# A state-space layer with a mixture of experts on one core: experts of the next-to-last row placed mostly within the last row's slot, and stages at moments of their own on ScalarE and VectorE

## The reference

```python
h = layernorm(x) * (1 + ca) + sa                  # modulation from silu(c) @ wmod
x = x + ga * state_space(h)
h = layernorm(x) * (1 + cb) + sb
x = x + gb * experts(h)

def state_space(x):
    xn = layernorm(x) * norm_scale + norm_bias
    xb, z = split(xn @ W_in)                      # 512 channels each
    xb = silu(conv3(xb)); dt = softplus(xb @ W_dt + b_dt)
    B, C = xb @ W_B, xb @ W_C                     # 16 states
    h_t = exp(dt_t * A) * h_(t-1) + dt_t * x_t * B_t
    y_t = sum over states of h_t * C_t
    return x + ((y + D * xb) * silu(z)) @ W_out

def experts(x):                                   # 16 experts, inner width 128, 4 of them used per token
    w = routing weights from sigmoid(x @ gate_weight), top 2 of 4 groups, top 4 experts
    return sum over e of w[:, e] * (silu(x @ gate[e]) * (x @ up[e])) @ down[e]
```

## Time and profile before

| | us |
|---|---|
| median of 3 runs | 2831.6 (2829.8 to 2836.8) |
| the profiled execution | 2827.4 |
| its span, first to last instruction | 2825.6 |
| VectorE busy | 2430 (86%) |
| TensorE busy | 2399 (85%) |
| GpSimd busy | 2238 (79%) |
| ScalarE busy | 1564 (55%) |
| start of the first scan | 95.5 |

### The profile page before, as it was taken

One profiled execution on the slowest core, in us unless ns is written; L12 is line 12 of the kernel. 1 busy time (PEld: TensorE's weight loads), 2 busy tenths in 40 slices (PEclk: granted clock), 3 DMA queues, 4 the chain that ended last, 5 costly groups with the idle time before them and its releaser, 6 DMA issues.

```text
span 2825.6 us, 29196 instructions
## 1 busy us (share of the span) xinstructions
PE 2398.6 (85%) x9004; PEld 1685.0 (60%) x9004; DVE 2430.4 (86%) x2482; ACT 1564.0 (55%) x2945; POOL 2237.5 (79%) x1563
## 2 busy tenths in 40 slices
PE   3445698989989898997989899898989989898899
PEld 1212466666756666675666667566666756666678
DVE  2678899989989898999989899998989899898932
ACT  3555665556556556656665665566566556655311
POOL 1577888888888888888888888888888888887922
PEclk7667899999989899999999899998989999899999
DMA  4699899999999999999999999999999999998921
GB/s 111 180 225 232 227 235 242 231 235 237 239 234 231 234 228 237 236 239 234 236 241 232 232 238 235 234 234 234 238 232 235 237 233 237 231 241 220 258 70 49
DMA packets 354510, 626.19 MB, mean 222 GB/s; under 512 B 51488, under 2 KB 162080, under 8 KB 354352
## 3 DMA queue, kind: packets, MB, share of 16 engines
q0 software_dynamic: 72960, 243.30, 45.3%
q1 hardware_dynamic: 281392, 381.01, 42.9%
HBM read 379.25 MB, written 10.06 MB: 138 GB/s over the span
## 4 chain that ended last, share of the span: by engine, by line
PE 40%; DVE 23%; issue 12%; POOL 9%; ACT 8%; DMA 7%; SPq 1%; DVEq 0%; POOLq 0%; ACTq 0%
DVE hbank L700 13%; PE wbank L477 13%; PE mbank L489 6%; PE wbank L419 4%; PE wbank L379 4%; POOL unit L1167 4%; PE wbank L505 4%; PE wbank L367 3%; DMA w_all<-w_scratch 2%; DMA w_scratch<-rows_out 2%; PE wbank L502 2%; DMA gsum<-unit 2%; DVE unit L714 2%; ACT z L823 2%; DVE act L678 2%
## 5 line engine op out<-in xcount | busy, mean ns | idle before, releaser
L1167 POOL TENSOR_TENSOR unit<-dtx,b_bc 128x1024 f32<-128x1024 f32 x512 | 1358.7, 2663 | 10.5 <-DMA b_bc<-bc_scratch 6.3
L700 DVE TENSOR_TENSOR_SCAN hbank<-hbank,unit 128x1024 f32<-128x1024 f32 x512 | 1173.3, 2292 | 103.3 <-ACT hbank L997 94.4
L997 ACT ACTIVATE hbank<-dt,a_neg 128x512 f32<-128x512 f32 x1024 | 669.2, 681 | 332.7 <-DVE unit L714 298.8
L489 PE MATMUL mbank<-down_t,act 128*128 128x256 f32 x2048 | 536.1, 402 | 57.1 <-POOL act L1135 31.2
L1179 POOL DMA_DIRECT2D gsum<-unit x448 | 452.7, 1010 | 161.4 <-DVE unit L714 75.4
L714 DVE TENSOR_TENSOR unit<-hbank,c_bc 128x1024 f32<-128x1024 f32 x448 | 545.8, 1218 | 22.3 <-DMA c_bc<-bc_scratch 1.4
L1135 POOL TENSOR_TENSOR act<-act,w_all 128x512 f32<-128x512 f32 x256 | 360.0, 1406 | 252.2 <-DVE act L678 228.2
L477 PE MATMUL wbank<-h_t,gate_t 128*128 128x256 f32 x2048 | 496.3, 386 | 24.1 <-DVE act L678 12.7
L489 PEld LDWEIGHTS mbank<-down_t,act 128*128 128x128 f32 x2048 | 402.1, 200 | 162.2 <-issue 62.6
L477 PE MATMUL wbank<-h_t,up_t 128*128 128x256 f32 x2048 | 486.9, 381 | 12.9 <-DVE gz L587 11.2
L477 PEld LDWEIGHTS wbank<-h_t,gate_t 128*128 128x128 f32 x2048 | 387.7, 192 | 128.6 <-DVE act L678 27.1
(11 more groups left out here) (122 smaller groups left out, 2400.9 us busy)
## 6 DMA issues: line engine op xcount, KB each, us to landing
gsum<-unit POOLq DMA_DIRECT2D x448, 512.0 KB, 7.5
b_bc<-bc_scratch SPq DMA_DIRECT2D x512, 256.0 KB, 6.3
c_bc<-bc_scratch SPq DMA_DIRECT2D x512, 256.0 KB, 5.5
w_all<-w_scratch SPq DMA_DIRECT2D x256, 256.0 KB, 5.0
ht<-in_L_attn_x_dram SPq DMA_DIRECT2D x16, 512.0 KB, 8.5
w_out<-in_L_attn_W_out_dram SPq DMA_DIRECT2D x16, 512.0 KB, 10.1
ht<-in_L_attn_x_dram POOLq DMA_DIRECT2D x16, 512.0 KB, 10.2
out_dram<-xt SPq DMA_DIRECT2D x16, 512.0 KB, 3.3
```

The lines of the kernel that those rows point to most:

```text
L489: m = eng.matmul(mbank[:, u * H:(u + 1) * H], act[:, (n - 1) % MOE_RING, j, u * P:(u + 1) * P], down_t[:, e, :], start=(e == 0 and u == 0) ...
L700: eng.tensor_tensor_scan(h, h, unit[:, g % RING, :, :].rearrange("p a t -> p (a t)"), 0.0, ALU.mult, ALU.add).then_inc(scanned, 1)
L997: eng.activation(hbank[g % HB][:, a, :], dt[:, 2 * q + a, :], ACT.Exp, scale=a_neg[:, 2 * q + a, n:n + 1]).then_inc(decayed, 1)
L1167: eng.tensor_tensor(unit[:, g % RING, :, :], dtx[:, 2 * q:2 * q + 2, :], b_bc[:, s:s + 1, :].to_broadcast([P, 2, T]), ALU.mult).then_inc(d ...
```

## The change

The change only moves instructions within the queues; the instructions themselves stay the same.

- Row 14's experts are spread over moments 37 to 107 of slot 15 in place of 38 to 131 (`SHORT_EXPERTS_AT`). Those of row 15 start at tail moment 43 in place of 33, behind everything that is placed in the tail.
- `streams`: `load_gb`, `stats`, `weigh`, `load_wo`, `load_ga`, `scale_wo`, `gates` and `silu_last` get other moments. `last_streams` too.
- `streams` takes a table of delays for single stages on one engine. ScalarE takes up `project` 2 moments later and `rows_bc` 1 later, VectorE takes up `mix1` 1 earlier; all other entries are 0.
- SP takes up the experts' DMAs (loads of `w_all`, output of a row) 4 moments late in place of 3 (`W_LAG`).

```diff
@@ -103,11 +103,16 @@
     SLOWEST = 1e-25
     MOE_RING = 2
     EXPERTS_AT = (38, 131)
+    SHORT_EXPERTS_AT = (37, 107)
     EP = E // 2
-    LAST_EXPERTS_AT = (33, 134)
+    LAST_EXPERTS_AT = (43, 124)
     HALVES = 4 * (E + 1)
     EARLY = 4
     ACT_LAG, DVE_LAG, POOL_LAG, SP_LAG = 1, 2, 3, 3
+    W_LAG = 4
+    ACT_LATE = {"project": 2, "stats": 0, "turn": 0, "gates": 0, "silu_first": 0, "silu_last": 0, "rows_bc": 1,
+                "step_sizes0": 0, "step_sizes1": 0, "turn_in": 0, "norms": 0, "weigh": 0}
+    DVE_LATE = {"gates": 0, "silu_first": 0, "silu_last": 0, "mix0": 0, "mix1": -1, "pick": 0}
     TAIL = 14
     HT = T // 2
     W2 = 2 * H
@@ -270,23 +275,25 @@
 
             return q if q < 2 else 2 + (q - 2) + 2 * (row % 2)
 
-        def streams(slot, stage):
+        def streams(slot, stage, late):
+
 
             behind, coming = slot - 1, slot + 1
             plan = [] if slot else [("chunks", 0, 2 * (len(chunks) - EARLY), 4, 40)]
             if behind >= 0:
-                plan += [("mix1", behind, 4, 11, 14), ("load_gb", behind, 1, 54, 56),
-                         ("project", behind, 4, 15, 24), ("stats", behind, 5, 20, 26),
-                         ("turn", behind, 4, 27, 30), ("pick", behind, 5, 30, 32), ("weigh", behind, 2, 36, 37)]
-            plan += [("step_sizes1", slot, 9, 1, 7), ("load_wo", slot, 1, 24, 30), ("load_ga", slot, 1, 23, 26), ("scale_wo", slot, 1, 47, 47),
-                     ("scale_h", slot, 2, 56, 58), ("gates", slot, 9, 36, 42),
+                plan += [("mix1", behind, 4, 11, 14), ("load_gb", behind, 1, 56, 58),
+                         ("project", behind, 4, 15, 24), ("stats", behind, 5, 22, 26),
+                         ("turn", behind, 4, 27, 30), ("pick", behind, 5, 30, 32), ("weigh", behind, 2, 34, 36)]
+            plan += [("step_sizes1", slot, 9, 1, 7), ("load_wo", slot, 1, 33, 42), ("load_ga", slot, 1, 31, 46), ("scale_wo", slot, 1, 48, 48),
+                     ("scale_h", slot, 2, 56, 58), ("gates", slot, 9, 35, 41),
                      ("mix0", slot, 4, 55, 62)]
             if coming < NB:
                 plan += [("load_x", coming, 1, 24, 29), ("norms", coming, 12, 31, 45), ("turn_in", coming, 2, 48, 55),
-                         ("silu_first", coming, 6, 57, 60), ("silu_last", coming, 6, 61, 65),
+                         ("silu_first", coming, 6, 57, 60), ("silu_last", coming, 6, 61, 66),
                          ("rows_bc", coming, 3, 81, 83),
                          ("step_sizes0", coming, 9, 73, 79)]
-            return [Steps(stage[name](row), n, first, final) for name, row, n, first, final in plan if name in stage]
+            return [Steps(stage[name](row), n, first + late.get(name, 0), final + late.get(name, 0))
+                    for name, row, n, first, final in plan if name in stage]
 
         def first_row(stage, begun=None):
 
@@ -298,13 +305,16 @@
         def last_streams(stage):
 
             last = NB - 1
-            plan = [("mix1", last, 4, 5, 5), ("project", last, 4, 6, 6),
-                    ("stats", last, 5, 6, 8), ("turn", last, 4, 16, 18), ("load_gb", last, 1, 21, 26),
-                    ("pick", last, 5, 16, 16), ("weigh", last, 2, 24, 25)]
+            plan = [("mix1", last, 4, 5, 5), ("project", last, 4, 5, 5),
+                    ("stats", last, 5, 6, 8), ("turn", last, 4, 18, 19), ("load_gb", last, 1, 3, 11),
+                    ("pick", last, 5, 13, 18), ("weigh", last, 2, 18, 25)]
             return [Steps(stage[name](row), n, first, final) for name, row, n, first, final in plan if name in stage]
 
         def experts_of(row, gen):
-            return Halves(gen(row), HALVES, *EXPERTS_AT) if 0 <= row < NB else None
+            if not 0 <= row < NB:
+                return None
+
+            return Halves(gen(row), HALVES, *(EXPERTS_AT if row < NB - 2 else SHORT_EXPERTS_AT))
 
         def experts_at(older, young, moment):
 
@@ -779,7 +789,7 @@
-                beside = streams(slot, stage_of) if run else last_streams(stage_of)
+                beside = streams(slot, stage_of, DVE_LATE) if run else last_streams(stage_of)
...
@@ -1036,7 +1046,7 @@
-                beside = streams(slot, stage_of) if run else last_streams(stage_of)
+                beside = streams(slot, stage_of, ACT_LATE) if run else last_streams(stage_of)
...
@@ -1370,7 +1380,7 @@
-                beside = streams(slot, stage_of)
+                beside = streams(slot, stage_of, {})
...
@@ -1378,7 +1388,7 @@
-                    experts_at(older, young, moment - SP_LAG)
+                    experts_at(older, young, moment - W_LAG)
...
```

More of the change, by code:

```diff
@@ L533, in _ @@
                 run = slot < NB
-                beside = streams(slot, stage_of) if run else last_streams(stage_of)
+                beside = streams(slot, stage_of, {}) if run else last_streams(stage_of)
                 young = experts_of(slot - 1, experts) if run else Halves(
```

1 line of the change is left out of this document (removed).

## The result

| | before | after |
|---|---|---|
| median of 8 runs each | 2829.95 (2823.09 to 2836.82) | 2839.38 (2834.62 to 2845.04) |
| ratio, with its 95% interval | | 1.0036 [1.0023, 1.0049] |
| span of the profiled execution | 2825.6 | 2836.5 |
| VectorE, TensorE busy | 2430, 2399 | 2430, 2382 |

What follows compares the result with a forecast made beforehand. VectorE was taken as nearest its limit, with everything near one, waiting mainly for ScalarE's decay. Slots 1 to 14 -6.3, slot 15 +3.65 and tail -7.8 gave -10.4 us: median 2821.2, range 2794 to 2837.

Steps and rivals of the forecast that it cites:

- `W_LAG` 4: SP's queue, k 12 to 17: w_scratch leaves some 1.6 us earlier, so the first w_all's wait of 1.03 goes.
- `project` and `stats`: k 8 to 10: decays run before project's second half, the apply comes earlier; gain 1.15 us a slot, bounds 0 to 2.3.
- Its signs: What would show the k 8 to 10 gain: scan 9 without wait and scan 10 waiting 2.3.
- Gates and `w_scratch`: k 12 to 17: first apply 2.1 later behind gate 1's tanh, about 1.4 absorbed; +0.7 a slot, bounds -1.05 and +2.1.
- The wait of scan 17: Sign for k 12 to 17: scan 17, which waited 1.05, would wait 1.5 to 2.
- first rival: Gates' order costs nothing, earlier w_scratch removes scan 17's wait; a slot gains 2.2, total 2797; chance 0.19.
- `w_out`: 512 KB load moved from k 11 to k 15: taken at nothing, bounds 0 and +2.2.
- third rival: GpSimd, k 15 to 19: moved w_out load makes an add wait 2.33; a slot costs 1.65 more, 2851; chance 0.18.
- Slot 15: Row 14's denser experts put 7 more VectorE operations of 0.68 us there: +4.8 us, bounds +2 and +8.
- The tail: After the last scan: transposes gain 2.0, w_all 5.8 more; down matmuls 7.8 us earlier, bounds -4 and -9.
- fourth rival: Tail: TensorE's clock at half for 17 us loses 8.5 us of work, 4.8 reaching the end; 2826; chance 0.12.

Runs made afterwards that it cites:

- u_wlag: The changed kernel with W_LAG 3 in place of 4, all else kept: 2809.90, ratio 0.9941 to the kernel before.
- u_gates: The changed kernel with gates and weigh back at their old moments: 2807.82, ratio 0.9935 to the kernel before.
- only_wlag: The kernel before with W_LAG 4 alone: 2836.36, ratio 1.0045.
- split_lag: The changed kernel with gates and weigh at old moments, SP lag 4 only for the older row's experts, 3 for the young row's: 2777.40, ratio 0.9831 to before.
- u_gates_wlag: The changed kernel with both the gates and weigh moments and W_LAG undone: 2789.32, ratio 0.9874 to the kernel before.
- only_gates: The kernel before with only the gates and weigh one moment earlier: 2839.24, ratio 1.0052.
- u_wo: The changed kernel with load_wo, load_ga and scale_wo at their old moments: 2843.15, ratio 1.0057 to the kernel before.

## Why the prediction was wrong, step by step

**The step that failed: `W_LAG` 4.** The prediction followed the experts' DMAs into one place, k 12 to 17, and found a gain. But the number holds for every moment of SP, and it moves 16 loads of `w_all` a row. For those of the young row, at k 26 to 31, no work was named, and no cost: their term in the sum is nothing, without a reason. The prediction did ask who waits for the adds beside a moved load, but only for `w_out`, the one load of 512 KB, where nothing came of it, and not for the 256 KB loads, of which there are 256. The price is 2.16 us a slot at k 1, 14 x 2.16 = 30 us (27 by the ratios of after and u_wlag). With that one number back, the rest of the change gives 2809.90, faster than the forecast.

**`project` and `stats`: right, with a gain beside it that was not foreseen.** Forecast 1.15 a slot, bounds 0 to 2.3. k 4 to 10 are 2.62 shorter, but the runs divide this into 1.21 for `project` and `stats`, 1.21 for the wait for the logits behind the clock at `turn`, and 0.20 for the small moves. So the term itself was met. Its signs were met in part: scan 9 is without a wait (1.10 before), but scan 10 waits 1.54 and not still 2.30, since in the profile of slot 8 TensorE's line 431 comes 0.5 earlier against scan 8 and `drive` takes 2.35, not 2.63; some of it is lost again, to a 0.33 wait at line 681 among others. The second 1.21 the prediction did not look at. It called VectorE's waits other than that for the decay far smaller; the second of them, `r_ch` with 19.6 us, is 1.5 a slot, as much as its terms.

**Gates and `w_scratch`: the sum nearly right, but not as two terms that add.** Forecast +2.1 for the order of the gates, -1.4 for the earlier loads, together +0.7. The runs have +1.66 (after against u_gates) and -0.83 (only_wlag against before) or -0.68 (split_lag against u_gates_wlag); together they gave +0.95. But with lag 3 the gates cost only 1.00 to 1.08 (only_gates against before, u_wlag against u_gates_wlag), and with the new gates lag 4 gives only 0.10 (u_wlag against after). The later apply makes the expert multiply late by itself, so that its wait for `w_all` is gone with lag 3 too; it was not the earlier load that absorbed it. So `W_LAG` 4 had nothing left to gain here. The wait of scan 17 was to be 1.5 to 2 and is 1.30 to 1.35 in each slot, from 1.05 in slot 8 of before. With lag 4 and the old gates (u_gates) scan 17 has no wait above 0.24: the first rival's mechanism is real too, but only without the new gates.

**k 19, not foreseen: +0.64.** k 19 has two values, 7.2 and 8.6; the higher goes with a granted clock of 0.58 to 0.67 behind the start of scan 18. Before has the higher one in 2 of 13 slots. The other kernels with the old gates have it in 0 to 5, those with the new gates in 6 to 10, after in 8. It goes with the gates, though not in each slot; by what way, no run shows.

**`w_out`: taken at nothing, and nothing it is.** The third rival was slower by a wait at k 16 to 18; u_wo rules it out. The case ended on that rival's side of zero, and by its kind of wait (an add that waits for one beside a moved load, and GpSimd's queue behind it), but for another load and in another place.

**Slot 15: right in the means, though not in this profile.** 7 more operations of 0.68 on VectorE, 4.8 us, were forecast. VectorE has 38 operations of the two lines in slot 15 where it had 31, exactly 7 more, and the means of all profiles give +4.7. In the profiled execution of after it was 0.4: VectorE's idle time in the slot is 9.3 us there, against 12.0 in before and 10.4 to 15.4 in the other kernels with the new experts.

**The tail: 134.7, forecast 131.8.** Timeline of after behind the last scan, which ends at 2701.85; answers to the earlier trace rows:

```profile
2711.37 1.02 PE L512 MATMUL wbank<-xb,diag_d 128*128 128x512 f32 x2
...
2733.68 1.97 PE L361 MATMUL wbank<-ident,z 128*128 128x128 f32 x8 [3.85 <-ACT z L833]
...
2736.61 3.57 PE L449 MATMUL wbank<-router_t,h_t 128*128 128x16 f32 x16 [0.96 <-ACT h_t L971]
...
2745.45 1.01 PE L361 MATMUL wbank<-ident,w_tok 128*16 128x128 f32 x4 [5.28 <-DVE w_tok L668]
2746.26 3.62 PE L487 MATMUL wbank<-h_t,gate_t 128*128 128x256 f32 x8
...
2747.11 0.32 SPq L1296 DMA_DIRECT2D w_scratch<-rows_out  x1
2748.70 14.01 SPq L1318 DMA_DIRECT2D w_all<-w_scratch  x5
...
2752.42 1.27 POOL L1145 TENSOR_TENSOR act<-act,w_all 128x512 f32<-128x512 f32 x1 [20.90 <-DVE act L688]
...
2754.90 1.89 PE L499 MATMUL mbank<-down_t,act 128*128 128x256 f32 x8
```

Three things differ from the forecast. First, TensorE has row 14's last halves still ahead of the products of `mix` (2711.37, 9.5 after the end of the last scan; before 5.5), and `project` and the apply come 3.1 later; the forecast left the apply where it was. Second, the clock is at half from 2732.7 to 2749.8:

```profile
2732.70:2749.80 17.10, 9.88 (x37) 8.45 (x38) 4.33 (x29) 3.28 (x6) 0.00 (x0) 0.50 0.12 32
```

The logits take 3.57 and not 1.93, the first gate group 3.62 and not 1.89. That is the fourth rival, with its 17 us. The Trainium skill ("TensorE: Matmul & The Clock Gate", section "Why this matters for your kernels") wants no idle gaps between bursts; the trace agrees, as the half clock sets in during the idle time of 3.85, while the tail of before has none above 0.65 in the 57 us behind its last scan and stays at 1.00. Third, and against these two, `w_scratch` lands after 1.6 and not 3.7. Together `w_all` leaves 46.9 after the last scan and not 43.8, and the first down matmuls come 53.05 after it, 4.8 earlier than before and not 7.8. How the missing 3.0 divide among the three, no run shows; the rival had 4.8 for the clock alone.

**The sum.** In place of 14 x -0.45 + 3.65 - 7.8 = -10.4 the profiled executions have +13.8 (slots 0 to 14), +0.4 and -4.9, and 1.6 ahead of the first scan: +10.9. The range failed because it was spread over the named places only; an edit of one number that moves 16 loads a row had no width of its own.

## What to carry to other kernels

When one constant shifts a whole class of instructions in a queue, list every place in the period where that class occurs and what each passes there, above all the waits of the queue: a load that slips behind a wait comes out in one bunch with what stood behind that wait. Look at who reads or reuses the buffer of the transfer that runs beside it, not only at who waits for the moved one. And split such a constant by the users it serves: here its two halves had opposite signs, and the split was worth 12 us over undoing it.

## What the hardware showed that I had not expected

- An accumulating add of 512 KB landed after 6.2 us, and after 9.3 with one load of 256 KB more in the bunch beside it (medians over 13 slots 5.7 and 8.6). The whole DMA traffic was the same.
- Idle times of TensorE of 1.9 to 3.2 us at the start of a slot went with some 3.4 us at a granted clock of 0.50, in 7 of 13 slots of after, and each cost 1.70 us at k 1; in u_gates the clock stayed at 1.00 beside 2.3 and 2.6. Idle for 2.71 at k 10 in before, the clock was at half in 10 of 13 slots. With 3.85 in the tail, and more idle times in the stretch, it stayed at half for 17 us.
- More matmuls made the kernel faster: one group of eight more in each of 14 rows, 0.2% less time, since the clock stayed up (by intervals that just touch).
- `w_scratch` (a write of 32 KB) landed after 1.6 us in the tail of after, where the DMA engines are nearly idle (0.12), against 3.5 to 5.4 in its slots and 3.7 in the tail of before.
